# A graph network layer on one core: edge sums through a DRAM spill, scattered by POOL while the node stage runs, and both lists taken from the highest down

## The reference, cut to what matters

```python
deg = jnp.maximum(jnp.zeros((n,), x.dtype).at[dst].add(1.0), 1.0)
edge_weight = (deg[src] * deg[dst]) ** (-DEG_POWER)              # DEG_POWER = 0.5
edge_msg = jax.nn.relu(edge_attr @ W1e + b1e) @ W2e + b2e
messages = (x[src] + edge_msg) * edge_weight[:, None]
agg = jax.ops.segment_sum(messages, dst, num_segments=n)
combined = (1.0 + gin_eps) * x + agg
h = jax.nn.relu(combined @ W1n + b1n) @ W2n + b2n
out = h + x
out = out * jax.lax.rsqrt(jnp.mean(out * out, axis=-1, keepdims=True) + RMS_EPS) * rms_w
return out                                                       # the layer
x = _layernorm(x + layer(...), axis=-1)                          # the result
```

## Time and profile before

| what | value |
|---|---|
| median of 3 runs | 1855.87 us (1836.1 to 1866.65) |
| span of the profiled execution | 1621.4 us |
| own time of the profiled execution | none is shown; the median less the span is 234.5 us |
| PE, DVE, ACT, POOL busy | 85%, 80%, 65%, 81% of the span |
| DMA | 275.61 MB, 170 GB/s over the span |
| mean granted TensorE clock | 0.921 of 2.4 GHz |

### The profile page before, as it was taken

The page is one execution under the profiler, slowest core; times in us unless marked ns, Lnnn a source line. Parts: engine busy times, 40 slices in busy tenths (PEclk is TensorE's granted clock), DMA queues, the critical chain, the costliest instruction groups (busy, mean ns, idle before and its releaser), DMA issues. The chain is left out here.

```text
span 1621.4 us, 33827 instructions
## 1 busy us (share of the span) xinstructions
PE 1376.2 (85%) x7563; PEld 865.4 (53%) x7563; DVE 1294.2 (80%) x4160; ACT 1050.1 (65%) x3889; POOL 1309.6 (81%) x2146
## 2 busy tenths in 40 slices
PE   7995899888878888887878781499999999999993
PEld 4553455444434344443434340377777777777772
DVE  8999798767766766676666672099999999999998
ACT  7995254444444344344344342299999999999997
POOL 7777777777777777777777777369999999999997
PEclk9998899988999898899988895699999999999997
DMA  9999332222222222222222411436777777677763
GB/s 345 378 376 387 117 97 68 68 79 80 67 67 67 69 88 70 67 67 67 80 80 68 157 42 40 145 131 245 291 264 289 264 279 277 267 291 267 290 254 152
DMA packets 63860, 275.61 MB, mean 170 GB/s; under 512 B 17737, under 2 KB 20211, under 8 KB 39344
## 3 DMA queue, kind: packets, MB, share of 16 engines
q1 hardware_dynamic: 38066, 230.80, 38.1%
q0 software_dynamic: 25136, 43.60, 9.2%
q10 hardware_dynamic: 590, 0.53, 0.1%
HBM read 154.37 MB, written 128.19 MB: 174 GB/s over the span
## 5 line engine op out<-in xcount | busy, mean ns | idle before, releaser
L600 POOL DMA_INDIRECT xs<-in_x,src_x x391 | 393.5, 1006 | 119.3 <-issue 104.8
L607 POOL DMA_INDIRECT agg_scratch<-scaled,sca_i x390 | 392.8, 1007 | 118.8 <-issue 106.3
L1157 PE MATMUL bank<-digits,picks 128*128 128x512 f16 x1568 | 414.4, 412 | 0.0
L731 ACT ACTIVATE scaled<-sums,dd 128x128 f32<-128x128 f32 x390 | 124.5, 390 | 442.8 <-DMA agg_scratch<-scaled,sca_i 442.8
L641 POOL TENSOR_SCALAR xsc<-xn,rms 128x128 f32<-128x128 f32 x784 | 277.5, 371 | 61.9 <-issue 18.1
L963 DVE SCALAR_TENSOR_TENSOR sums<-sums,cont,weights 128x128 f32<-128x128 f32 x391 | 135.1, 345 | 235.8 <-issue 218.2
L943 DVE SCALAR_TENSOR_TENSOR picked<-iota_h,src_lo,bank 128x512 f16<-128x512 f16 x392 | 288.6, 737 | 9.1 <-PE bank L1157 8.2
L779 ACT ACTIVATE squares<-res 128x128 f32<-128x128 f32 x784 | 257.6, 437 | 0.0
L1157 PEld LDWEIGHTS bank<-digits,picks 128*128 128x128 f16 x1568 | 165.0, 105 | 172.5 <-issue 49.9
L655 POOL TENSOR_SCALAR on<-z,neg_mean,rstd 128x128 f32<-128x128 f32 x564 | 244.3, 443 | 0.0
L1214 PEld LDWEIGHTS bank<-w2n,hn 128*128 128x128 f32 x1568 | 205.8, 191 | 70.5 <-issue 64.6
(11 more groups left out here) (153 smaller groups left out, 2336.1 us busy)
## 6 DMA issues: line engine op xcount, KB each, us to landing
agg_scratch<-zeros SPq DMA_DIRECT2D x48, 1024.0 KB
xn<-in_x SPq DMA_DIRECT2D x48, 1024.0 KB, 8.8
out<-on SPq DMA_DIRECT2D x48, 1024.0 KB, 4.9
ag<-agg_scratch SPq DMA_DIRECT2D x47, 1024.0 KB, 6.8
highq<-src_high_scratch SPq DMA_DIRECT2D x24, 512.0 KB, 3.9
ea<-in_edge_attr SPq DMA_DIRECT2D x21, 512.0 KB, 3.7
xs<-in_x,src_x POOLq DMA_INDIRECT x391, 2.7
agg_scratch<-scaled,sca_i POOLq DMA_INDIRECT x390, 2.2
```

What stands on the lines that cost most here:

```text
L600: pool.indirect_dma_start(out=xs[:, b % XS, j, :], out_offset=None, in_=x, in_offset=bass.IndirectOffsetOnAxis(ap=src_x[:, t:t + 1], axis= ...
L607: pool.indirect_dma_start(out=agg_rows, out_offset=bass.IndirectOffsetOnAxis(ap=sca_i[:, t:t + 1], axis=0), in_=scaled[:, b % SR, j, :], i ...
L1157: last = pe.matmul(ps[COUNTS[tile]][:, :], picks[:, s, c, tile * P:(tile + 1) * P], digits[:, c, :, :].rearrange("p d l -> p (d l)"), star ...
```

## The change

The edges are cut into G = 7 groups of 56 columns, the group of the highest destinations first; each partition owns a run of 56 edges in each group. The padding is at the lowest edges. In each group 55 columns are scattered and the last ones (`tails`) joined across partitions by `same` (now 128 x 128 for each group), one matmul, and one accumulating scatter for each group (`join`). `scaled` is no longer scattered from: ACT stores it into a DRAM scratch, `sums_scratch`, on its own queue (`store_sums`), and POOL reloads it in pieces of 14 columns into a ring of two (`refill`) and scatters from there. POOL issues all gathers first; 150 of the 392 columns are handled beside the gathers and the rest after them, while the node stage already runs. `BESIDE` is 150.

The node stage takes blocks of 2048 consecutive nodes from the highest down. A block's `ag` is loaded when as many groups are joined as reach it, a number that DVE computes from the last destination of each group (`waits_i`) and SP reads into a register. In the first 84 steps (`ALONE` = 21 blocks) POOL has no part: DVE makes `z` from `xn`, `rms` and the product with four scalar-tensor-tensor operations, and finishes three of four tiles. From step 84 the work is divided as before. The rings of `xn` and `ag` have three blocks; a slot of `xn` is free when `z` of the block three before is made. The degree table is split by the low part of the node number: 16 matmuls a batch have 391 columns instead of 512, two `picks` operations instead of four. The lists are made before the counting; their rows are spread over partitions through DRAM instead of PE. The node stage and the edge stage are written out without loops.

```diff
-    XS = 40
+    G, GB = 7, 14
+    GT = GB * TB
...
-    XR, AR = 4, 4
+    XR, AR = 3, 3
+    ALONE = 21
+    SA = ALONE * SPB
+    sums_d = nc.dram_tensor("sums_scratch", (RELOADS * P * RB, D), f32)
...
+            def load_x(i):
+                need(sp, z_ready, (i - XR + 1) * SPB)
+                sp.dma_start(xn[:, i % XR, :, :], in_group_order(x, i)).then_inc(xn_in[i % XR], 16)
+            def load_sums(i):
+                joins = sp.value_load(waits_i[0:1, i:i + 1], min_val=1, max_val=16 * G)
+                need(sp, cT_done, (i - AR + 1) * SPB)
+                sp.wait_ge(fin_added, joins)
+                sp.dma_start(ag[:, (i + 1) % AR, :, :], in_group_order(agg_d, i)).then_inc(ag_in[(i + 1) % AR], 16)
...
+            for i in range(BLOCKS + OUT_LAG):
+                if 2 <= i < BLOCKS:
+                    load_sums(i)
+                if XR <= i < BLOCKS:
+                    load_x(i)
+                C, o = i - OUT_LAG, (i - OUT_LAG) % OR
...
+                    sp.dma_start(in_group_order(out, C), on[:, o, :, :]).then_inc(out_sent[o], 16)
...
+            def refill(q):
+                for s in range(SR):
+                    pool.wait_ge(stored[s], spilled(s, -(-(q + 1) * RB // TB)))
+                need(pool, scattered[q % 2], 16 * sent(q))
+                n = of_block(q)
+                pool.dma_start(reload[:, q % 2, 0:n, :].rearrange("p t d -> p (t d)"),
+                               bass.AP(sums_d, q * P * RB * D, [[RB * D, P], [1, n * D]])).then_inc(reloaded[q % 2], 16)
...
+            def scatter(t):
+                q, c = t // RB, t % RB
+                if c == 0:
+                    pool.wait_ge(reloaded[q % 2], 16 * (q // 2 + 1))
...
+                if c == RB // 2 and q + 1 < RELOADS:
+                    refill(q + 1)
+                if t % GT == FIN_LAG and t > GT:
+                    join(t // GT - 1)
...
+            BEFORE, BESIDE = 6, 150
+            for b in range(XS, BATCHES):
+                gather(b)
...
+                done, parts = max(b - XS - BEFORE, 0), BATCHES - XS - BEFORE
+                if b == XS + BEFORE:
+                    refill(0)
+                for t in range(done * BESIDE // parts, (done + 1) * BESIDE // parts if b >= XS + BEFORE else 0):
+                    scatter(t)
+            for t in range(BESIDE, T):
+                scatter(t)
+            join(G - 1)
...
+            for n in range(SA, STEPS + 15):
+                node_step(n)
...
+            def store_sums(b):
+                act.wait_ge(scaled_ready, b + 1)
+                for j, n in spills(b):
+                    q, c = (b * TB + j) // RB, (b * TB + j) % RB
+                    act.dma_start(bass.AP(sums_d, (q * P * RB + c) * D, [[RB * D, P], [1, n * D]]),
+                                  scaled[:, b % SR, j:j + n, :].rearrange("p j d -> p (j d)")
+                                  ).then_inc(stored[b % SR], 16)
...
+                    for c in range(2):
+                        for d in range(2):
+                            last = pe.matmul(ps[COUNTS[tile]][:, 0:PICK], picks[:, b % 2, c, tile * P:(tile + 1) * P],
+                                             table[:, c, d, :], start=c == 0 and d == 0, stop=c == 1 and d == 1)
...
+                    if m < SA:
+                        dve.wait_ge(rms_ready, m + 1)
+                        for j in range(TB):
+                            last = dve.scalar_tensor_tensor(z[:, v, j, :], xn[:, xsl, h + j, :], rms[:, s, j:j + 1],
+                                                            xsc[:, m % 2, j, :], ALU.mult, ALU.add)
...
+                m = n - 18
+                if 0 <= m < SA:
+                    finish(m)
```

More of the change, by code:

```diff
@@ L366, in need, with run @@
                 eng.wait_ge(s, at(value))
[L368 to L373 removed]
+        def run(eng, total, unroll, step, peel=0):
             rounds = total // unroll - peel
[L377 removed]
+            for n in range(unroll):
                 step(n, n % unroll)
[L379 removed]
+            with eng.Fori(1, rounds) as i:
@@ L443, in build @@
[L443 to L451 removed]
+            return list(range(reached(n), min(reached(n + 1), STEPS)))
@@ new lines, in _ @@
+            dve.tensor_tensor(groups(new), here, before, ALU.not_equal)
+            dve.tensor_tensor(g3(cont), here, before, ALU.is_equal)
+            dve.tensor_scalar(far, gidx, -BIG, None, ALU.add)
+            link(dve.tensor_tensor(groups(eqn), here, after, ALU.is_equal))
+            dve.tensor_tensor(fst, gidx, new, ALU.mult)
+            link(dve.scalar_tensor_tensor(left, eqn, -1.0, far, ALU.add, ALU.mult))
+            for r in range(G):
+                last = dve.tensor_tensor_scan(start[:, r * GT:(r + 1) * GT], fst[:, r * GT:(r + 1) * GT],
+                                              fst[:, r * GT:(r + 1) * GT], 0.0, ALU.max, ALU.max)
@@ L829, in _ @@
+            link(last)
+            dve.tensor_copy(ends[:, 0, :], dst_f[:, :, GT])
+            dve.tensor_copy(ends[:, 1, :], groups(start)[:, :, GT - 1])
+            dve.tensor_reduce(ends[:, 2, :], groups(left), AXIS.X, ALU.max).then_inc(ends_ready, 1)
+            link(dve.scalar_tensor_tensor(groups(sca_f), groups(eqn), SKIP, here, ALU.mult, ALU.add))
+            dve.tensor_copy(sca_i[:, :], sca_f)
             dve.wait_ge(iota_set, 1)
```

1182 lines of the change are left out of this document (612 added, 570 removed).

## The result

| | us |
|---|---|
| kernel before, median of 4 runs | 1852.06 (1836.1 to 1866.65) |
| changed kernel, median of 4 runs | 2038.93 (2036.07 to 2085.93) |
| ratio, 95% interval | 1.100, 1.092 to 1.109 |
| profiled execution of the changed kernel: own time, span | 2036.07, 2034.3 |
| the kernel before once more, profiled (b0_before_again): own time, span | 1862.77, 1861.0 |

Slower by 10%, where 9.3% faster was forecast. The last row of the table is half of the explanation. Between a span and its execution's own time lie 1.8 us, not 234.5: the trace that the forecast was read from, with its span of 1621.4, is of an execution that none of the timed ones resembles. The order of events had to be read again, in a trace of the kernel before that belongs to its time.

A forecast was written before the change was run, and what follows sets the result against it. The prediction took POOL's 781 indirect transfers to bound the edge stage. It summed 757 to the first `res`, 341, 318, 21 and 12 to a 1449 us span, plus 234.5 outside: 1684 us, range 1655 to 1798.

The forecast's parts named there:

- So the edge stage is POOL issuing 781 indirect transfers: Edge stage before the change: 391 gathers and 390 scatters, one each 1.30 us, make POOL the bound.
- 234.5 us lie around the span. I keep these as they are: Outside the profiled span of 1621.4 us: 234.5 us up to the median of 1855.87, added unchanged to the forecast.
- An edge batch of 5.4 us: Edge stage without POOL's limit: shorter picks bring a batch to 5.4 us, bounds 5.3 and 6.17.
- rival C: Edge stage: the batch stays at 6.17 us, last message at 803, 1747 us in all; chance 0.08.
- 15 us more to the first message: Start and setup: loads, masks over 7 groups and list of waits move the first message from 189.9 to 205 us.
- 17 us from the last message to the first `res`: Between edge and node stage: 10 us of tail and 7 of first node work, first `res` at 757; 33 us won.
- 84 steps at 4.06: Node steps without POOL: 4.06 us each on DVE, 341 us where 239 are spent now, 102 given back.
- POOL done at 1078, needed at 1099: Node stage: POOL finishes remaining scatters, reloads and joins before DVE reaches its first step with POOL, margin 21 us.
- rival D: Node stage: POOL is late at step 84, by slow reloads (1711 us) or DVE's finishing operations (1729); chance 0.12.
- So it just fits: Node stage, three-slot `xn` ring: landing of 5.2 us fits 5.4 beside POOL; 12 us added for misses and clock.
- Rival A: Node stage: the three-slot `xn` ring binds, 1723 us at 6.8 us landing, up to 1798; chance 0.14.
- Rival B: Node stage: `xn` landings of 10.0 us or more make it slower than before, 1955 us at 12; chance 0.06.

The follow-up runs named there:

- before_pause_all: Kernel before with a waited-for 128x32 POOL memset ahead of every gather and scatter, all through; 1960.6 us.
- after_rest2: Changed kernel with a waited-for 128x32 POOL memset ahead of every second indirect transfer, ring of three kept; 1610.5 us.
- plain_no_scatter: Changed kernel with gathers replaced by plain DMAs of rows in order on SP's queue and the 385 scatters left out; 1428.7 us.
- alone_two: Changed kernel with ALONE = 2 in place of 21, so 8 node steps without POOL instead of 84; 1931.9 us.
- rest2_ring4: Changed kernel with a waited-for 128x32 POOL memset at every second indirect transfer and four `xn` slots; 1645.2 us, ratio 0.877 to the kernel before.
- after_rest1: Changed kernel with a waited-for 128x32 POOL memset ahead of every gather and every scatter; 1748.1 us.
- plain_rows: Changed kernel with POOL's gathers replaced by as many plain DMAs of `x` rows in order from SP's queue, scatters kept; 1667.5 us.

## Why the prediction was wrong, step by step

- **"So the edge stage is POOL issuing 781 indirect transfers"**: the step that failed. It is true of the execution that was traced and of before_pause_all, not of the timed ones without a rest. There POOL is busy 62% and not 77, because its transfers, following one another, hold PE, DVE and ACT up, and POOL then waits for them. The change takes no indirect transfer away, it moves 235 scatters behind the gathers. As long as the others are held up there is nothing to overtake: the ring of gathered rows stays full, the last gather is issued at 872.9 us, 40 batches ahead of its message, and all 385 scatters fall into an edge stage of 10.9 us a batch, where it was 10.3. That a batch with 7 transfers goes slower than one with 6.4 fits their order: from 500 to 560 us the kernel before issues 7 to 13 in a row between two waits, the changed kernel 15 to 21, and behind the gathers 14 at a time. Of the 585 us between the forecast span of 1449 and 2034.3, 557 lie ahead of the last message (740 forecast, 1297.3 measured).
- **"234.5 us lie around the span. I keep these as they are"**: false, 1.8 us. It was the sign that trace and time don't belong together. An unexplained eighth of the time was carried through the sum instead of being made a rival, with halts in every stage as its price. The forecast of 1684 consists of a span of 1449 that no run with the gathers reached and of a constant that doesn't exist; that it lies near after_rest2's 1610 is chance.
- **An edge batch of 5.4 us**: right, where nothing halts it: 5.46 in plain_no_scatter, and clock 1.00. So were the shorter picks, and rival C is dead.
- **15 us more to the first message**: too much. Where nothing halts the engines it is 195.8 us (plain_no_scatter) against 189.9.
- **17 us from the last message to the first `res`**: right, 13.9 (1297.3 to 1311.2). The gain is smaller than the 33 forecast, since the kernel before takes 31.7 there in b0_before_again, not 50.
- **A reload of 1.3 us on POOL**: its issue took 0.60 us. Its landing is in no row.
- **84 steps at 4.06**: right, 298.0 / 76 = 3.92. But "where 239 are spent now: 102 us given back" was to be paid out of the edge stage. POOL had its last scatter out at 1347.9, 37 us into the node stage. That is within the first eight of the 84 steps, and the rest was pure loss, which alone_two shows.
- **POOL done at 1078, needed at 1099**: the edges held POOL back as POOL held them. With the rest the two meet as drawn: in after_rest2 POOL was through at 1253 and step 84 waited some 40 us for it, rival D's place.
- **"So it just fits", the ring of three**: short by 0.18 us a step beside POOL, where 12 us were allowed for small misses, clock and all. Rival A was right in kind; at 20 to 27 us it is about an eighth of the loss.
- **Rival B**, the one that ended slower, was the wrong mechanism: the sign came from the halts, for which no chance was set aside.

The Trainium skill (SBUF — State Buffer, Who interferes with whom) has one way by which POOL's transfers and the other engines meet: DVE and POOL share ports, and one keeps the other out. Here PE and ACT stop as well, in one instant with DVE, and by that section PE and ACT share no port with POOL; it does not explain these rows.

**Open.** Through what POOL's transfers reach the others is not shown. Late semaphores fit the first of the two listings, a starved fetch or issue of instructions the second, and I had no edit that parts them. That the trace of b0_before_again holds 12144 semaphore updates and the first one, of the same program, 23846 means that many a "remote" or "issue" may be a wait whose end was not recorded. Few updates alone are no halt: in the node stage both traces have about one to three instructions, and both run at 2.84 us a step. Whether the recording itself has a part in the halts is open: nearly all timed runs have a span and a clock on record too. Nor is it known why the very first trace has none of it, why a batch costs 7.7 us in rest2_ring4 and 6.3 in after_rest2, why the early batches of after_rest1 take 10, or what the gathers of 63 to 71 us are. plain_rows changed two things at once, the indirection and the issuing engine; that the pace hangs on the spacing rests on the runs with the rest.

## What to carry to other kernels

Set the span of a trace against the time of the very execution that it was taken from before reading anything else in it; if they differ by more than a few us, what is read may be true of that execution and of no timed one. Where POOL issues rows of indirect transfers, look whether the other engines have idle time that names no one, and try a short waited-for operation between the transfers: it costs an edit of five lines. Work that is moved off an engine is worth what the engine's waits say, and the work that is put elsewhere to make room (84 steps here) is paid in full whether or not the room was needed.

## What the runs showed of the hardware

- Indirect transfers of POOL that follow one another at 1.26 to 1.34 us hold PE, DVE and ACT up. In rows of four with a wait behind, counting loses 22% of its speed (6.85 us for 5.34); scatters in threes and fours with 1.3 to 1.5 us behind cost the edge batch 0.5 us (6.67 for 6.17); in a row of 160 the edge stage does four batches in 184 us, some 46 us each for 5.4.
- A POOL memset of 128x32, waited for (0.14 to 0.24 us; 0.4 to 1.0 us then lie between two transfers instead of 0.3) takes most of it away: 5.7 us a batch with one before every transfer (but 10 from 200 to 290 us, beside gathers alone), 6.3 to 7.7 before every second, 10.2 before every third, 10.9 with none.
- A POOL memset of 128x256 (0.43 us) behind each gather also takes the stops out of counting, but the two DVE operations beside it take 0.75 and 0.55 us for 0.42; one of 128x32 (0.15 us) lengthens them by 0.01.
- Where POOL's transfers hold the others up, a wait can go on 1.7 us after what it waited for, and in the edge stages PE, DVE and ACT stop together for up to 9 us at a time.
- The same program ran without any of it in one execution (span 1621.4); none of its timed executions took under 1836 us.
